# A two-layer metaformer kernel on one core: norm and ordering of pass one write their middle values to a PSUM bank

## The reference

```
xn     = (x - mean_c x) / sqrt(var_c x + 1e-6)           # norm over the 96 channels
x_feat = in_proj(xn);  x_conv = silu(dwconv3x3(x_feat))
sim    = <x_conv / |x_conv|, centre / |centre|>          # |.| not under 1e-12
order  = argsort(-sim)                                   # of the 2304 pixels
xs     = x_conv in that order, forwards and backwards
h_t    = exp(dt_t A) h_{t-1} + dt_t x_t B_t;  y_t = C_t h_t   # scan, 16 states, both directions
y      = back in pixel order, layernorm;  local conv + batchnorm + silu;  gate;  out_proj
```

## Time and profile before

| What | Value |
|---|---|
| median of 3 runs | 20241.44 us (20240.05 to 20243.45) |
| the profiled execution's own time | 20238.29 us |
| its span, first to last instruction | 20236.5 us |
| TensorE busy | 15651.5 us, 77% |
| VectorE busy | 12811.8 us, 63% |
| GpSimd busy | 11733.7 us, 58% |
| ScalarE busy | 9077.8 us, 45% |
| mean granted TensorE clock | 0.84 |

### The profile page before, as it was taken

How to read it: one execution, slowest core, us unless ns; L and a number is a source line. 1 busy time by engine, 2 the same in 40 slices (tenths; PEclk the granted TensorE clock), 3 DMA queues, 4 the chain that set the end, 5 groups by cost and what they waited for, 6 DMA issues and landing times. The chain is left out here.

```text
span 20236.5 us, 211579 instructions
## 1 busy us (share of the span) xinstructions
PE 15651.5 (77%) x66607; PEld 8562.7 (42%) x66607; DVE 12811.8 (63%) x14009; ACT 9077.8 (45%) x16440; POOL 11733.7 (58%) x9604
## 2 busy tenths in 40 slices
PE   7878787878787878787875677777777777777777
PEld 3333333333333333333332344444444444544444
DVE  5888888888888888888886344444444444444443
ACT  4555555555555555555553333333333333333332
POOL 3666666666666666666665355555555555555555
PEclk8888888888888888888887688888888888888887
DMA  2333333333333333333333455444454454544454
GB/s 62 87 91 87 91 87 90 89 87 89 89 88 92 85 92 86 91 87 90 89 88 91 114 144 141 137 140 139 140 145 135 139 143 140 142 139 138 140 141 120
DMA packets 1294658, 2230.12 MB, mean 110 GB/s; under 512 B 712841, under 2 KB 756125, under 8 KB 1281629
## 3 DMA queue, kind: packets, MB, share of 16 engines
q1 hardware_dynamic: 893022, 1086.35, 20.9%
q0 software_dynamic: 368640, 1076.24, 18.6%
q10 hardware_dynamic: 32256, 56.64, 0.9%
HBM read 1493.27 MB, written 271.92 MB: 87 GB/s over the span
## 5 line engine op out<-in xcount | busy, mean ns | idle before, releaser
L1480 POOL DMA_INDIRECT G<-corners,idx x5184 | 4920.2, 949 | 4202.2 <-issue 1618.1
L1270 POOL TENSOR_TENSOR hc<-h,crep 128x768 f32<-128x768 f32 x2304 | 4175.2, 1814 | 3743.0 <-DVE h L1072 2250.6
L711 PE MATMUL ps<-hc,sel 128*96 128x512 f32 (+1 forms) x9216 | 3951.5, 557 | 590.4 <-POOL hc L1270 435.5
L1513 PE MATMUL ps<-ident,G 128*96 128x128 f32 x20736 | 2950.4, 298 | 350.0 <-PEq L161 140.2
L1056 DVE TENSOR_TENSOR ps<-dxr,ps 128x768 f32<-128x768 f32 x2304 | 2186.0, 949 | 1363.4 <-PE ps L700 1266.4
L1513 PEld LDWEIGHTS ps<-ident,G 128*96 128x96 f32 x20736 | 2636.2, 140 | 886.8 <-issue 802.4
L1072 DVE TENSOR_TENSOR_SCAN h<-decay,carry,ps 128x768 f32<-128x768 f32 x1536 | 2776.7, 1808 | 164.2 <-ACT decay L894 95.1
L711 PEld LDWEIGHTS ps<-hc,sel 128*96 128x96 f32 x9216 | 1552.8, 184 | 2534.3 <-issue 1782.0
L1773 DVE TENSOR_TENSOR G<-G,ps 128x1536 f32<-128x1536 f32 (+1 forms) x1152 | 2235.6, 1942 | 1.1
L894 ACT ACTIVATE decay<-dtr,a_neg 128x768 f32<-128x768 f32 x2304 | 2120.5, 926 | 234.6 <-DVE h L1072 214.5
L700 PE MATMUL ps<-bq,pick 96*128 96x512 bf16 (+1 forms) x4608 | 1285.5, 365 | 1126.9 <-DVE h L1072 783.3
(11 more groups left out here) (215 smaller groups left out, 21889.6 us busy)
## 6 DMA issues: line engine op xcount, KB each, us to landing
crep<-c_rows SPq DMA_DIRECT2D x3072, 96.0 KB
dtr<-rel SPq DMA_DIRECT2D x2304, 96.0 KB
dxr<-mag SPq DMA_DIRECT2D x2304, 96.0 KB
corners<-prow SPq DMA_DIRECT2D x1536, 72.0 KB
G<-corners,idx POOLq DMA_INDIRECT x5184
x_in<-in_x SPq DMA_DIRECT2D x32, 864.0 KB
local_all<-local_c ACTq DMA_DIRECT2D x192, 144.0 KB
sim<-sorted_rows SPq DMA_DIRECT2D x32, 864.0 KB, 6.0
```

The lines of the kernel that those rows point to most:

```text
L711: m = pe.matmul(wide(BY, C)[:, a:b], Wt["sel"][:, cg, :], hc[:, v % HC, a:b], start=(v % ROUND == 0), stop=(v % ROUND == ROUND - 1))
L1270: pool.tensor_tensor(hc[:, s % HC, :], h[:, s % HR, :], crep[:, g % CRING, :], ALU.mult).then_inc(S["s_weighted"], 1)
L1480: pool.indirect_dma_start(M["G"][:, slot(t, which), k, :], None, table, bass.IndirectOffsetOnAxis(idx[:, t, k:k + 1], 0)).then_inc(S[f"p_g ...
L1513: m = pe.matmul(ps[0:C, BT + n % 2, (k % 4) * P:(k % 4 + 1) * P], M["G"][:, slot(v, which), k, q * C:(q + 1) * C], ident[:], is_transpose= ...
```

## The change

In the norm, the two Newton steps write over the variance in PSUM (`var`, columns 0 to 383 of bank 6) instead of the SBUF tile `newton`, and the last multiplication reads it there. In the ordering, lengths (19 columns from 384) and distances (18 columns from 448) stand in unused columns of the same bank instead of the SBUF tiles `rlen` and `dist`. `rlen` still carries the sum of squares to ScalarE's square root and back, and `dist` still holds the last result, which TensorE and the comparison read. The arithmetic, its order and all waits are the same.

```diff
-                    step(dve.scalar_tensor_tensor(out=newton, in0=ps[0:C, BS, 0:CH], scalar=1e-6, in1=newton,
+                    var = ps[0:C, BS, 0:CH]
+                    step(dve.scalar_tensor_tensor(out=var, in0=var, scalar=1e-6, in1=newton,
                                                   op0=ALU.add, op1=ALU.mult))
-                    step(dve.scalar_tensor_tensor(out=newton, in0=newton, scalar=-3.0, in1=inv,
+                    step(dve.scalar_tensor_tensor(out=var, in0=var, scalar=-3.0, in1=inv,
                                                   op0=ALU.add, op1=ALU.mult))
                     centred = xn[0:C, 1 + 8 * c:9 + 8 * c, 1:1 + W]
                     dve.scalar_tensor_tensor(out=centred, in0=centred, scalar=-0.5,
-                                             in1=newton.rearrange("p (r x) -> p r x", x=W), op0=ALU.mult,
+                                             in1=var.rearrange("p (r x) -> p r x", x=W), op0=ALU.mult,
...
+                length, apart = ps[:, BS, CH:CH + NT + 1], ps[:, BS, CH + P // 2:CH + P // 2 + NT]
...
-                    step(dve.tensor_scalar(rlen[:], rlen[:], 1e-12, None, ALU.max))
+                    step(dve.tensor_scalar(length, rlen[:], 1e-12, None, ALU.max))
-                    dve.tensor_scalar(flag[:], rlen[:], 1e-12, None, ALU.is_le)
-                    step(dve.reciprocal(rlen[:], rlen[:]))
-                    step(dve.tensor_tensor(unit[:], rows[:], across(rlen[:]), ALU.mult))
+                    dve.tensor_scalar(flag[:], length, 1e-12, None, ALU.is_le)
+                    step(dve.reciprocal(length, length))
+                    step(dve.tensor_tensor(unit[:], rows[:], across(length), ALU.mult))
...
-                    step(dve.tensor_reduce(dist[:], unit[:, 0:NT, :], AX.X, ALU.add))
+                    step(dve.tensor_reduce(apart, unit[:, 0:NT, :], AX.X, ALU.add))
...
-                    step(dve.tensor_tensor(dist[:], dist[:], flag[:, 0:NT], ALU.add))
+                    step(dve.tensor_tensor(apart, apart, flag[:, 0:NT], ALU.add))
                     step(dve.tensor_scalar(flag[:, CEN_TILE:], flag[:, CEN_TILE:], -1.0, 1.0, ALU.mult, ALU.add))
-                    dve.tensor_scalar(dist[:], dist[:], flag[:, CEN_TILE:], None, ALU.mult).then_inc(S["o_dist"], 1)
+                    dve.tensor_scalar(dist[:], apart, flag[:, CEN_TILE:], None, ALU.mult).then_inc(S["o_dist"], 1)
```

## The result

| | before | after |
|---|---|---|
| median | 20242.44 us (20240.05 to 20258.4, 4 runs) | 20088.86 us (20077.01 to 20102.61, 4 runs) |
| profiled execution (span) | 20238.29 us (20236.5) | 20077.01 us (20075.2) |
| mean granted clock of TensorE | 0.840 | 0.851 |
| mean of images 1 to 29 | 339.8 us | 334.6 us |

The ratio is 0.9923, 95% interval 0.9906 to 0.994: 154 us less, where 58 were forecast and 20135 was the lower end of the range. Run again on two more occasions, each on a chip of its own, the changed kernel stood at 0.9917 [0.99, 0.9933] and 0.9929 [0.9913, 0.9946] to the kernel before.

What follows compares the result with a forecast made beforehand. It took GpSimd's queue as the path in steps 46 to 56 and part of 5 to 16, TensorE from 57. Gains of 41.3 and 16.8 us, together 58, gave 20183 us; range 20135 to 20238.

Steps and rivals of the forecast that it cites:

- The clock: TensorE at half clock after idling: one more such stretch an image gives 20234 (chance 0.08), two 20285 (0.04).
- Step 57: nothing: Norm in step 57: lifting its hold gains nothing, as step 58's replication comes from a fully busy TensorE.
- The forms and their holds: VectorE's two-SBUF-input instructions and L1122 exclude GpSimd's work; with PSUM operands L1104, L1122, L1136 take 0.54, 0.18, 0.16 us.
- PSUM operands at no price: 25 instructions an image with PSUM operands cost nothing extra, bound 0.06 us each either way.
- the rule it weighed: Skill page: `tensor_tensor` doesn't stall GpSimd's descriptor generation, so the 1.90 us gather in step 10 would stay.
- the first rival: GpSimd's DMA instructions don't gain; only 21 us saved, 20220 us, chance 0.15.
- Steps 5 to 16: Ordering: GpSimd's queue is the path in 13 images, TensorE comes late in 17; 41.3 us in all.
- The gather's 0.95 us: Step 10: with L1126 on one SBUF input, the gather takes 0.95 instead of 1.90 us on GpSimd's path.
- The 0.75 us for L1136 in 17 images: Steps 13 and 14: L1136 no longer held, 0.75 of 0.82 us gained where TensorE comes late; bounds 0 and 0.82.
- Steps 46 to 56: GpSimd is the path; freeing the norm in steps 48 and 54 gains 0.56 us an image, 16.8 us in all.

Runs made afterwards that it cites:

- unit_sbuf: Changed kernel with the reciprocals written back to SBUF, so the product of rows and reciprocals reads two SBUF operands: 18260.1 us, 0.9968 to the kernel before.
- centre: Changed kernel with the middle row copied to PSUM for the subtraction and distances moved onto the lengths' columns: 18188.78 us, 0.9929 to the kernel before.
- norm_only: Kernel before with only the three edits of the norm, the ordering left as it was: 20149.63 us, 0.9937 to the kernel before.
- dist_sbuf: Changed kernel with the ordering's distances left in SBUF, lengths and reciprocals still in PSUM: 20152.69 us, 0.9922 to the kernel before.
- hold57: Changed kernel with the norm's chunk of step 57 in SBUF as before: 20154.2 us, 0.994 to the kernel before.
- shift_once: Kernel before with one VectorE memset of 1900 elements ahead of pass one: 20292.32 us, 1.0002 to the kernel before.
- after_delay: Changed kernel with a VectorE memset of 600 elements at each image's end: 18195.5 us, 0.9933 to the kernel before.
- centre_warm: Changed kernel with the middle row in PSUM and unread matmuls added in steps 10 and 12: 20149.11 us, 0.9922 to the kernel before.
- warm: Changed kernel with 16 and 8 unread matmuls added on TensorE in steps 10 and 12: 20115.86 us, 0.9906 to the kernel before.
- after_again: Changed kernel unedited, run again on another occasion: 18165.64 us, 0.9917 to the kernel before.

## Why the prediction was wrong

- *The clock* is the step that failed. It was there as a rival that can only cost, and in the forecast's own range as "up to 1 us either way": noise around nothing. It brought 2.6 us an image, on one side: 1.6 in steps 0, 1, 26, 27 and 64, where nothing was changed, and some 1.0 of the 1.32 in steps 57 to 59; with part of the 0.67 below it may be up to 3.3. That is 79 to 99 us in 30 images, more than the 58 us of the sum. The low stretches lie on fixed multiples of 3.41 us, so that a saving of two to three microseconds moves every later step to another phase, and images settle at whole numbers of intervals: 338 to 341 us before, 334.5 after.
- *"Step 57: nothing"* failed as well, at the same point. It held that the replication of step 58 comes from a TensorE that is fully busy. TensorE was full because the low clock stretched it; at full clock its centring waits for the held norm. In 16 of the 29 images of the kernel before the step was right as it stands (14.38 us with the hold or without). In the 10 at full clock, and in nearly all of the changed kernel's, the hold is worth 0.82 us: 25 us in all at the new phases, an estimated 8 at the old ones.
- *The forms and their holds* were right: 0.56, 0.17 and 0.18 us, PSUM operands at no price (2.05 against 2.06, 1.95 against 1.95), the gather of 1.90 gone and that of 2.54 kept. With that the rule it weighed falls for this case: the first rival's 20220 did not come, and unit_sbuf and centre show that a second SBUF input alone makes the gather long or short.
- *Steps 5 to 16*: forecast 1.38 us an image, measured 1.63. The gather's 0.95 us is right to 0.01 in the 13 images in which GpSimd ends the stretch (40.43 to 39.48) and in norm_only. The 0.75 us for L1136 in 17 images was under-sized or was another thing: the 16 images of that kind lose 1.2 us more, 0.67 in the mean of all. dist_sbuf puts L1136's hold back at no cost, but for the two images that meet a low stretch there, which cost 1.2. So the term, too, hangs on the clock, and whether the hold, the clock or only both together make it stays open.
- *Steps 46 to 56*: 0.56 against 0.54.
- By its own mechanisms the sum was thus near: 0.95 + 0.54 + 0.3 for step 57, and 0 to 0.67 for L1136, make 1.8 to 2.5 us an image, an estimate, where it had 1.94 and 5.14 were measured. The near agreement of 1.38 and 1.63 is partly luck, for the same reason.
- hold57 and unit_sbuf show the same from the other side: one hold of 0.79 us put back makes the image 1.8 us longer, gathers of 1.66 us put back make it 3.0 longer.
- *What stays open*: which length an image settles at was not derived, only observed. That the low stretches set the lengths rests on shift_once and on images of the same code whose steps take one time or another according to them (step 64: 3.56 or 5.2 us); no run set them by hand. Of four kernels in which it was meant to be steered (shift_once, after_delay, centre_warm, warm) one did better than the changed kernel.

## What to carry to other kernels

Ask of each instruction beside a busy GpSimd how many of its inputs lie in SBUF: an operand moved to PSUM costs nothing here and frees both engines, and it is worth its time where GpSimd's queue is the path. Before a wait is put at nothing because TensorE is full there, look at the granted clock of that stretch: an engine that is full at half clock has slack at full clock, and the wait behind it then counts. And where a loop's body repeats many times, compare the lengths of its single rounds: a saving can come back doubled or not at all, according to where the low clock falls next.

## What the runs showed of the hardware

- A VectorE instruction with two SBUF inputs that meets a product of GpSimd is held until that product ends and then takes its own time (4.68 us instead of 2.05 in unit_sbuf, 2.99 instead of 0.56 in hold57). An indirect DMA instruction of GpSimd that starts within such a VectorE instruction ends 0.82 to 0.87 us behind it (1.52, 1.90, 2.52, 2.62 us instead of 0.94 to 0.98). With one input in PSUM neither is longer. The other order is free: the gather at 5046.15 was under way when L1126 started, and neither took longer (0.98 and 2.06 us). Two forms with one SBUF input are held too: L1122 (3.41 us) and the copy of ranks (0.78). The Trainium skill (SBUF — State Buffer, Who interferes with whom) infers the opposite for descriptor generation under `tensor_tensor`; for the gathers of this kernel the measurement decides. Whether they are held in writing descriptors or in reading their ranks from SBUF was not separated.
- The recorded granted clock changes only between 0.50 and 1.00, and only at whole multiples of 3.413 us from its first change, within 0.001 us, in all sixteen records (898 to 1700 stretches each), with images of 330 to 342 us.
- Pass one took the same time in all three profiled executions of the changed kernel (334.6 to 334.9 us an image), two of which ran on different chips; pass two did not. A stretch of it in the changed kernel's first run and in after_again:

```profile
11200.00:20000.00 8800.00, 6731.66 (x34017) 4291.67 (x34012) 3658.30 (x5416) 3186.30 (x7054) 4870.96 (x5132) 0.82 0.49 140
```
```profile
11200.00:18100.00 6900.00, 5716.14 (x34025) 3783.43 (x34023) 3670.91 (x5415) 3163.93 (x7055) 4909.22 (x5128) 0.93 0.63 178
```

The same work takes 8800 us at a granted clock of 0.82 and 140 GB/s, and 6900 us at 0.93 and 178 GB/s. Which of the two is the cause was not tested; ratios were taken within a chip.
